# A decoder layer on one core: VectorE's operands and results kept in PSUM, with a new order of steps and a new bank table

## The reference

```python
# 1. gated linear recurrence, C = 512
q = silu(x @ Wq1 @ Wq2)
f = sigmoid(x @ Wk1 @ Wk2)
a = exp(log_sigmoid(f)); k = 1 - a
h[t] = a[t] * h[t-1] + k[t] * (x @ Wv)[t]
o = q * h; o = o * rsqrt(mean(o*o) + 1e-6) * norm_w
x = layernorm(x + o @ Wo)
# 2. attention with 8 heads over ctx: softmax(q k / sqrt(32)) v,
#    the heads being groups of 32 tokens, q = x, k = v = ctx
x = layernorm(x + attention(x, ctx))
# 3. feed-forward, 1024 hidden
x = layernorm(x + (silu(x @ Wg) * (x @ Wu)) @ Wd)
```

## Time and profile before

| what | value |
|---|---|
| median of 3 runs | 181.44 us (180.5 to 182.04) |
| profiled execution, its own time | 181.35 us |
| its span, first to last instruction | 179.6 us |
| mean granted TensorE clock | 0.952 |
| TensorE busy | 155.6 us (87%) |
| VectorE busy | 130.3 us (73%) |
| ScalarE busy | 112.3 us (63%) |
| GpSimd busy | 85.1 us (47%) |

### The profile page before, as it was taken

One profiled execution on the slowest core, in us unless ns is written; L12 is line 12 of the kernel. 1 busy time (PEld: TensorE's weight loads), 2 busy tenths in 40 slices (PEclk: granted clock), 3 DMA queues, 4 the chain that ended last, 5 costly groups with the idle time before them and its releaser, 6 DMA issues.

```text
span 179.6 us, 4001 instructions
## 1 busy us (share of the span) xinstructions
PE 155.6 (87%) x1528; PEld 143.8 (80%) x1528; DVE 130.3 (73%) x214; ACT 112.3 (63%) x258; POOL 85.1 (47%) x95
## 2 busy tenths in 40 slices
PE   7964599627996989999999999999999999999960
...
DVE  3369978995599996696999968677726776436561
...
POOL 1259956999687564240628413242521314302701
PEclk9999669995899999999999999999999999999996
...
GB/s 183 327 409 407 314 58 0 0 58 81 100 2 4 0 5 58 4 0 0 4 2 58 4 0 5 0 0 4 0 0 62 2 4 0 58 4 0 0 58 58
DMA packets 5138, 10.47 MB, mean 58 GB/s; under 512 B 640, under 2 KB 1664, under 8 KB 5120
## 3 DMA queue, kind: packets, MB, share of 16 engines
...
HBM read 9.18 MB, written 1.05 MB: 57 GB/s over the span
## 4 chain that ended last, share of the span: by engine, by line
PE 65%; DVE 19%; issue 5%; ACT 3%; DMA 3%; SPq 1%; POOLq 0%; DVEq 0%; POOL 0%
PE banks L379 40%; PE banks L463 6%; PE banks L523 6%; DVE hid L731 5%; PE banks L450 3%; DMA prob<-wv 3%; PE banks L529 3%; PE banks L485 3%; DVE res L771 2%; DVE neg_top L800 2%; ACT numer L631 2%; DVE gat L739 2%; DVE mix L748 1%; DVE hid L727 1%; PE banks L495 1%
## 5 line engine op out<-in xcount | busy, mean ns | idle before, releaser
L951 POOL TENSOR_TENSOR g_lo<-gu,g_hi 128x512 fp32r<-128x512 f32 x15 | 19.8, 1324 | 40.4 <-ACT g_hi L673 40.3
L631 ACT ACTIVATE numer<-banks,neg_top 128x256 f32<-128x256 f32 x64 | 29.4, 484 | 6.7 <-DVE neg_top L800 6.7
L832 DVE SCALAR_TENSOR_TENSOR gu<-gu,banks 128x512 f32<-128x512 f32 x16 | 10.9, 684 | 17.4 <-ACT gu L665 17.3
L665 ACT ACTIVATE gu<-banks 128x512 f32<-128x512 f32 x16 | 9.6, 601 | 21.9 <-PE banks L379 21.7
L800 DVE TENSOR_REDUCE neg_top<-banks 128x4 f32<-128x1024 f32 x16 | 19.0, 1218 | 5.6 <-PE banks L450 5.5
L731 DVE TENSOR_TENSOR_SCAN hid<-dec,hid 128x256 f32<-128x256 f32 x16 | 20.3, 1308 | 0.3
L642 ACT ACTIVATE prob<-banks 128x1024 f32<-128x1024 f32 x16 | 16.2, 1022 | 4.7 <-PE banks L463 4.7
L379 PE MATMUL banks<-low_lo,w_high_hi 128*128 128x256 f32 x32 | 10.4, 326 | 9.2 <-DVE low_lo L716 9.2
L463 PE MATMUL banks<-ident,numer 128*128 128x128 f32 x128 | 16.0, 273 | 1.8 <-ACT numer L631 1.8
L523 PE MATMUL banks<-w_down_hi,g_hi 128*128 128x256 f32 x64 | 16.0, 285 | 0.0
L463 PEld LDWEIGHTS banks<-ident,numer 128*128 128x128 f32 x128 | 14.2, 140 | 2.0 <-issue 2.0
...
## 6 DMA issues: line engine op xcount, KB each, us to landing
...
```

The source lines that it names most:

```text
L631: ins = nc.scalar.activation(numer[:, n % 2, 2 * h + c, :], place["scores", b, i][:, 2 * h + c, :], ACT.Exp, bias=neg_top[:, 2 * i + h, c: ...
L832: nc.vector.scalar_tensor_tensor(out=v, in0=v, scalar=1.0, in1=ps[:, 0:2, :], op0=ALU.add, op1=ALU.mult).then_inc(gate_done, 1)
L951: nc.gpsimd.tensor_tensor(g[1][:, 2 * i:2 * i + 2, :], gu[:, n % 2, :].rearrange("p (k t) -> p k t", k=2), g[0][:, 2 * i:2 * i + 2, :], AL ...
```

## The change

What VectorE reads and writes is moved to PSUM in six places; steps get a new order on every engine, and results new banks.

- `recur`: (dec - 1) * value is written back into value's bank, and the scans read it there and write `hid`. The wait for the squares of the batch before stands in front of the scans, not of the product. One increment of `state_done` for two scans.
- `silu`: (gat + 1) * query is written back into query's bank, and `mix` reads it there.
- `add_mixed`, `weigh`, `add_down`: product and sum are written into the bank of mixed, context or down; statistics read that bank.
- `norm_apply` reads the bank and writes `res`.
- `freed_by`: value's bank is free after the scans, query's after `mix`, those of mixed, context and down after the normalisation. ScalarE's `query` waits for `silu_done`, `keep_inverse` for `weighed`.

```diff
-        freed_by = {"value": [kv_done], "decay": [tan1], "query": [silu_done], "scores": [exp_done],
-                    "turn_exp": [prob_kept], "hidden": [g_done], "down": [added[2]], "low": [low_lo],
-                    "squares": [sq_turned], "mixed": [added[0]], "inverse": [inv_spread], "context": [weighed],
+        freed_by = {"value": [state_done], "decay": [tan1], "query": [out_done], "scores": [exp_done],
+                    "turn_exp": [prob_kept], "hidden": [g_done], "down": [normed[2]], "low": [low_lo],
+                    "squares": [sq_turned], "mixed": [normed[0]], "inverse": [inv_spread], "context": [normed[1]],
...
+                kv = place["value", b, i]
-                nc.vector.scalar_tensor_tensor(out=hid[:, cs, :], in0=dec[:, cs, :], scalar=1.0, in1=place["value", b, i][:, :, :],
+                nc.vector.scalar_tensor_tensor(out=kv[:, :, :], in0=dec[:, cs, :], scalar=1.0, in1=kv[:, :, :],
...
-                    nc.vector.tensor_tensor_scan(hid[:, cc, :], dec[:, cc, :], hid[:, cc, :], 0.0, ALU.mult,
-                                                 ALU.subtract).then_inc(state_done, 1)
+                    ins = nc.vector.tensor_tensor_scan(hid[:, cc, :], dec[:, cc, :], kv[:, k, :], 0.0, ALU.mult,
+                                                       ALU.subtract)
+                ins.then_inc(state_done, 1)
...
+                gated = place["query", b, i]
-                nc.vector.scalar_tensor_tensor(out=gat[:, cs, :], in0=gat[:, cs, :], scalar=1.0, in1=place["query", b, i][:, :, :],
+                nc.vector.scalar_tensor_tensor(out=gated[:, :, :], in0=gat[:, cs, :], scalar=1.0, in1=gated[:, :, :],
...
-                nc.vector.tensor_tensor(mix[:, cs, :], gat[:, cs, :], hid[:, cs, :], ALU.mult).then_inc(out_done, 1)
+                nc.vector.tensor_tensor(mix[:, cs, :], gated[:, :, :], hid[:, cs, :], ALU.mult).then_inc(out_done, 1)
...
-                    ins = nc.vector.tensor_scalar(tile[:, t, :], tile[:, t, :], mv[:, n, t, 0:1], rstd[:, n, t:t + 1],
+                    ins = nc.vector.tensor_scalar(res[:, b, t, :], tile[:, t, :], mv[:, n, t, 0:1], rstd[:, n, t:t + 1],
...
+                total_ = place["mixed", b, 0]
-                    ins = nc.vector.scalar_tensor_tensor(out=x_i[:, t, :], in0=place["mixed", b, 0][:, t, :],
-                                                         scalar=rms[:, t:t + 1], in1=x_i[:, t, :],
+                    ins = nc.vector.scalar_tensor_tensor(out=total_[:, t, :], in0=total_[:, t, :],
+                                                         scalar=rms[:, t:t + 1], in1=res[:, b, t, :],
...
-                nc.vector.tensor_tensor(inv_b[:, :, :], place["context", b, 0][:, :, :],
-                                        inv_b[:, :, :], ALU.mult).then_inc(weighed, 1)
+                total_ = place["context", b, 0]
+                nc.vector.tensor_tensor(total_[:, :, :], total_[:, :, :], inv_b[:, :, :], ALU.mult).then_inc(weighed, 1)
-                nc.vector.tensor_tensor(res[:, b, :, :], res[:, b, :, :], inv_b[:, :, :], ALU.add).then_inc(added[1], 1)
+                nc.vector.tensor_tensor(total_[:, :, :], total_[:, :, :], res[:, b, :, :], ALU.add).then_inc(added[1], 1)
```

More of the change, by code:

```diff
@@ L56 @@
     "sp.w_low": [[0.7]],
-    "sp.xt": [[1.2], [1.7], [6.7], [7.7]],
-    "sp.w_high": [[2.2, 3.2]],
-    "sp.w_v": [[2.7]],
+    "sp.xt": [[1.2], [1.7], [4.7], [7.2]],
+    "sp.w_high": [[2.2, 2.7]],
+    "sp.w_v": [[3.2]],
     "sp.w_o": [[3.7]],
[L61 to L86, removed]
@@ L93 @@
[L93 removed]
+    "sp.ctx": [[5.2], [5.7], [14.57], [29.84]],
+    "sp.ctx_t": [[6.2], [9.2], [57.82], [84.67]],
+    "sp.x": [[6.7], [8.2], [21.19], [52.86]],
+    "sp.weights": [[7.7, 8.7, 9.7, 10.2, 11.41, 19.87]],
+    "sp.store": [[108.46], [124.73], [161.08], [167.75]],
+    "pe.low": [[5.32, 6.31], [7.02, 16.46], [26.41, 43.4], [52.26, 62.89]],
+    "pe.decay": [[7.83, 8.72], [12.82, 17.17], [31.57, 38.74], [64.03, 77.88]],
@@ new lines @@
+    "pe.query": [[9.43, 10.2], [25.7, 27.12], [48.85, 50.68], [77.18, 84.44]],
+    "pe.value": [[11.41, 13.63], [15.05, 17.88], [44.11, 46.47], [65.52, 85.17]],
+    "pe.squares": [[19.93], [34.6], [57.59], [94.77]],
+    "pe.mixed": [[21.9], [35.9], [58.11], [95.77]],
+    "pe.scores": [[35.12, 42.62], [55.0, 64.74], [81.42, 93.99], [111.72, 125.75]],
+    "pe.turn_exp": [[39.6, 41.57, 49.81, 51.39], [60.94, 62.02, 75.43, 76.3], [86.58, 93.12, 107.15, 108.02], [120.84, 121.71, 132.32, 133.19]],
@@ L94 @@
     "dve.w_low": [[3.73]],
     "dve.xt": [[5.32]],
[L96 to L103, removed]
@@ L136 @@
-    "turn_exp": [[4, 2, 2, 6], [2, 4, 2, 2], [6, 6, 0, 6], [0, 2, 0, 6]],
-    "inverse": [[4], [1], [6], [4]],
-    "context": [[1], [0], [7], [5]],
-    "turn_x": [[6], [4], [5], [4]],
-    "hidden": [[6, 4, 6, 4], [4, 6, 4, 4], [2, 6, 4, 2], [2, 6, 2, 4]],
-    "down": [[1], [4], [5], [2]],
+    "low": [[0, 1], [2, 5], [0, 7], [0, 4]],
+    "decay": [[3, 0], [5, 3], [2, 7], [0, 7]],
+    "value": [[3, 0], [2, 0], [6, 0], [4, 4]],
+    "query": [[4, 1], [4, 5], [1, 4], [6, 7]],
+    "squares": [[4], [3], [4], [4]],
```

123 lines of the change are left out of this document (73 added, 50 removed).

## The result

| | before | after |
|---|---|---|
| median, us | 180.97 (180.28 to 182.04) | 172.86 (172.69 to 173.80) |
| ratio, with 95% interval | | 0.9557 (0.9494 to 0.9621) |
| profiled execution, us | 181.35 | 172.81 |
| its span, us | 179.6 | 171.0 |
| mean granted clock of the span | 0.952 | 0.969 |

The forecast was 174.2 us (171.0 to 178.5), faster.

What follows compares the result with a forecast made beforehand. VectorE, waiting for GpSimd, paces 15 to 65 us; TensorE's work bounds it from 77.5 us. Hidden 0.0 at 67.5 + 95.1 + 2.1 + 1.5 = 166.2, tail 6.1 + 0.15, span 172.4, plus 1.75: 174.2 us (171.0 to 178.5).

Steps and rivals of the forecast that it cites:

- The excess goes: VectorE's waiting for GpSimd goes: sixteen scans from 1.308 to about 0.656 us, gated products from 0.991 to 0.69.
- Together 18 us of VectorE's time: Sum of VectorE time saved: scans 10.4, gated product 2.4, L815 1.9, normalisations 3.5 us.
- PSUM writes at no cost: 36 VectorE instructions now write PSUM: taken as zero, upper end 0.145 us each, 1.5 us for ten on the early path.
- A normalisation pair out of PSUM at 0.86: VectorE's normalisation pairs reading PSUM: 0.86 us against 0.73 undisturbed, +0.13 a pair, on the path only in the tail.
- The walk to scores 0.0: New order walked step by step from profiled durations: scores 0.0 starts at about 35.2 us against 45.17, 10.0 us gained.
- Then a new lateness: query 1.1: On ScalarE query 1.1 stands behind weights and low 2.0, done at 31.2 us; TensorE stands most of 27 to 33.
- Low 1.0 no longer stands behind recur and silu, so the stand goes: TensorE's stand at 15.7 to 20.2 us goes; it runs until 19.5, then waits about 1.5 us for the gated product.
- I take no gain ... hidden 0.0 at 67.5: Scores 0.0 to hidden 0.0 keeps its 32.3 us though the walk gives 31.2; hidden 0.0 at 67.5 us, 66.4 by the walk.
- Rival A: Only half the gain: GpSimd not the whole cause, or the stand for low 2.0 grows; 177 to 179 us, chance 0.16.
- B: Rival of more gain: hidden 0.0 at 66.4, no 0.50 clock behind the 27 us stand, no added idle; 170 us, chance 0.10.
- D: Rival of no effect: VectorE's second SBUF operand is not what waits, only order counts; 180 to 182 us, chance 0.04.
- Rival C: Slower: mixed, context and down banks held 3 to 4 us longer make nine TensorE steps wait; about 188 us, chance 0.04.

Runs made afterwards that it cites:

- e3_pool_writes: Kernel before, GpSimd's twelve reading subtractions for the feed-forward weights' low halves replaced by write-only fills: 180.11 us in one run.
- e6_low_query_early: Changed kernel, ScalarE's low 2.0 and query 1.1 moved ahead of the last weights, VectorE's low 2.0 ahead of norm1: 173.32 us, ratio 0.9604.
- e1_order_alone: New order and bank table with the operands and bank releases of the kernel before: 181.75 us, ratio 1.0054 against the kernel before.
- e2_scan_gate_old_order: Kernel before, only scans and gated product on their matmuls' PSUM banks; order, banks, sums and normalisations as before: 174.46 us, ratio 0.965.

## Why the prediction was right

The time of 172.86 lies in the range, and the cause is the one given: VectorE's instructions with two operands in SBUF waited for GpSimd. Step by step:

- **The excess goes** (forecast: scans at 0.65 to 0.70, L748 at 0.69): 0.674 and 0.692. `e3_pool_writes` shows that GpSimd's access to SBUF was the cause: with twelve of its reading subtractions replaced, the scans' median fell from 1238 to 692 ns, though VectorE's code was unchanged. GpSimd itself gained as well, which the forecast didn't count: busy 79.6 us where it was busy 85.1.
- **"Together 18 us of VectorE's time"**: too much; its busy time fell by 13.1 us (130.3 to 117.2). The scans (20.3 to 10.1), L748 (7.9 to 5.5) and L815 (4.7 to 2.8) gave what was forecast. The normalisations, put at 3.5 us, gave 0.9 (12.8 to 11.9): a pair takes 1.00 and not 0.86, and the sum set twice the mean of one, 1.15, against 0.86 of a pair in the timeline, where the two overlap. Only four of the twelve pairs before took over 0.9 us, and the eight at 0.71 to 0.74 got slower. The forecast of the time does not use the 18.
- **PSUM writes at no cost**: small, not zero. In place in PSUM against to SBUF: 690 against 665 ns (recur), 682 against 668 (silu), 486 against 468 (L785). 14 to 25 ns each, 0.2 us over the ten of the early path, far below the upper end of 0.145 us each.
- **A normalisation pair out of PSUM at 0.86**: it takes 1.00 (536 ns each). Too small by 0.14 us, which is the step taken from L781 as the nearest row. Here the Trainium skill (VectorE: DVE Perf Modes, "Why PSUM operands drop a tier") was nearer: the estimate by it was 0.27 over 0.73 us, and the trace agrees with 1.00. On the path this is 0.14 us in the tail and little more.
- **The walk to scores 0.0**: 35.2, seen 34.69. Its landmarks: recur 1.0 to 22.1 (22.6), low 1.1 at 22.5 (23.0), recur 1.1 to 25.3 (25.2), mixed to 27.2 (27.4), silu 1.0 to 28.6 (28.75), silu 1.1 to 32.6 (32.1), low 2.0 to 33.0 (32.5), x1_rest to 33.9 (34.0). That silu 1.1 came out within 0.5 us is partly luck, for two errors offset each other: "Then a new lateness: query 1.1", put at 31.2, was done at 30.44, and norm1, put at 29.0 to 29.8, ran from 29.8 to 30.8, since its root came late; silu 1.1 stood behind norm1 (in `e6_low_query_early`, with query 1.1 earlier, norm1 still waits 1.18 us). "Low 1.0 no longer stands behind recur and silu, so the stand goes" holds (`e1_order_alone`), but the stand goes with the old order too (`e2_scan_gate_old_order`), and without the operands its going was worth nothing. The credit in time belonged to the operands.
- **Scores 0.0 to hidden 0.0**: "I take no gain ... hidden 0.0 at 67.5" was the largest miss. The stretch took 31.7 us, between the walk's 31.2 and the 32.3 taken, and began 0.5 us earlier; hidden 0.0 came at 66.39, 1.1 us earlier than taken. That it agrees with the walk's 66.4 is chance: the two differences of 0.5 us cancel.
- **Behind hidden 0.0**: 95.1 + 2.1 = 97.2 us of work, 97.45 seen. "I put 1.5" of idle, 0.8 seen. So the whole miss: 1.1 us at hidden 0.0 and 0.7 of idle, less 0.25 of work, put the end of the last matmul at 164.65 against 166.2; the tail, 6.35 against 6.25, takes 0.1 back, and 1.4 us are left of the span, 171.0 against 172.4.
- **Clock and stand**: a stand of 5 us and a granted 0.50 in the 4.5 us behind it, as forecast. TensorE's wait for the gated product of the second half was put at 1.5 us and took 0.80.
- **Rival A** (half) is out by the result. Of **B**'s conditions hidden 0.0 at 66.4 came and no added idle came; the clock above 0.50 didn't, and that was worth the most. **D** is refuted as to the operands, yet for the order alone its number of 180 to 182 was right: 181.75.
- **Rival C** (banks held longer): TensorE waits 0.8 us in all behind 66.4 us, once, for ScalarE:

```profile
PE banks L379 <- ACT x2t_hi L656: 0.8, 1, 0.8
```

  not for a bank that a normalisation holds. "Evacuate promptly" (the Trainium skill, PSUM — Partial Sum Buffer, "Summary: rules for kernel authors") pointed the other way; this trace, with its new bank table, does not agree. TensorE waits for no held bank in front of 66.4 us either.
